# Weighted sums of two chunks over halves of 64 keys, beside scores and maxima on the other array tiles

## The reference

```
layer 0: window attention (7x7 windows, 8 heads of 8, cosine similarity, position bias), + x,
         group norm, relu; group norm, 64 -> 256 -> 64 perceptron, + h, group norm, relu  = z
layer 1: qkv = w_qkv z                    (4 heads of 16, n = m = 3136 positions)
         attn = softmax(q^T k * 16^-0.5)  (3136 x 3136 for each head and image)
         out = w_proj (v attn^T) + z
```

## Time and profile before

| | us |
|---|---|
| median of 3 runs (9116.72 to 9124.28) | 9118.54 |
| profiled execution, its own time | 9125.05 |
| its span | 9123.3 |
| TensorE matmuls busy | 8091.4 (89%) |
| VectorE busy | 7403.4 (81%) |
| ScalarE busy | 6195.0 (68%) |
| GpSimd busy | 792.9 (9%) |

### The profile page before, as it was taken

One profiled execution on the slowest core, in us unless ns is written; L12 is line 12 of the kernel. 1 busy time (PEld: TensorE's weight loads), 2 busy tenths in 40 slices (PEclk: granted clock), 3 DMA queues, 4 the chain that ended last, 5 costly groups with the idle time before them and its releaser, 6 DMA issues.

```text
span 9123.3 us, 325558 instructions
## 1 busy us (share of the span) xinstructions
PE 8091.4 (89%) x145928; PEld 2803.4 (31%) x145928; DVE 7403.4 (81%) x9252; ACT 6195.0 (68%) x13810; POOL 792.9 (9%) x677
## 2 busy tenths in 40 slices
PE   4798989989899898998989899898998989899897
PEld 2232323323233232323323233232332323233222
DVE  3788888878888788887888888788887888888884
ACT  1377667767667677676776677676776776767776
POOL 3100101001010010101001010010100101010000
PEclk8799999999999999999999999999999999999998
DMA  1201111020110201112011110201102011110110
GB/s 31 40 13 25 26 29 27 14 38 16 23 27 15 39 14 26 26 20 35 12 26 26 29 27 14 38 15 25 26 14 39 14 26 26 23 32 12 29 21 18
DMA packets 126086, 222.76 MB, mean 24 GB/s; under 512 B 60419, under 2 KB 92291, under 8 KB 124555
## 3 DMA queue, kind: packets, MB, share of 16 engines
q1 hardware_dynamic: 124690, 201.94, 12.3%
HBM read 67.50 MB, written 42.73 MB: 12 GB/s over the span
## 4 chain that ended last, share of the span: by engine, by line
PE 56%; DVE 27%; SPq 5%; DMA 4%; ACT 4%; issue 3%; POOL 0%; POOLq 0%; ACTq 0%; DVEq 0%
DVE small L949 22%; PE PS L1324 18%; PE PS L1311 15%; PE PS L1169 9%; ACT exps L842 3%; SPq L626 3%; PE PS L1210 3%; PE PS L1230 3%; DMA small<-scratch_att 1%; DVE small L988 1%; PE PS L1262 1%; PE PS L1271 1%; DMA tok_unit<-in_query_ident 1%; DMA scratch_att<-o_st 1%; PE PS L1200 1%
## 5 line engine op out<-in xcount | busy, mean ns | idle before, releaser
L842 ACT ACTIVATE exps<-PS 128x392 f32<-128x392 f32 x12800 | 5417.0, 502 | 2428.1 <-PE PS L1311 1972.0
L949 DVE TENSOR_REDUCE small<-PS 128x1 f32<-128x784 f32 x6400 | 5863.8, 965 | 895.7 <-PE PS L1169 864.5
L1311 PE MATMUL PS<-q_stack,k_stack 50*32 50x392 f16 x51200 | 3037.4, 338 | 383.7 <-DMA q_stack<-neg_rows 220.2
L1324 PE MATMUL PS<-exps,v_all 128*32 128x392 f32 x25600 | 2823.1, 516 | 11.6 <-ACT exps L842 6.6
L1169 PE MATMUL PS<-k_stack,q_stack 48*32 48x392 f16 x51200 | 2486.7, 342 | 374.3 <-DVE small L949 293.1
L1311 PEld LDWEIGHTS PS<-q_stack,k_stack 50*32 50x32 f16 x51200 | 989.1, 90 | 2528.1 <-ACT exps L842 1942.1
L1169 PEld LDWEIGHTS PS<-k_stack,q_stack 48*32 48x32 f16 x51200 | 771.2, 90 | 2039.0 <-DVE small L949 1551.9
L1324 PEld LDWEIGHTS PS<-exps,v_all 128*32 128x32 f32 x25600 | 518.8, 109 | 796.5 <-issue 491.5
L742 POOL TENSOR_TENSOR win_scores<-win_scores,small 128x784 f32<-128x784 f32 x256 | 385.1, 1506 | 1822.0 <-DVE small L1000 1822.0
L988 DVE TENSOR_REDUCE small<-PS 128x16 f32<-128x784 f32 x256 | 247.4, 966 | 187.1 <-PE PS L1210 187.0
L1210 PE MATMUL PS<-kmask,tok_unit 113*64 113x392 f32 (+1 forms) x2048 | 375.2, 502 | 19.7 <-DMA tok_unit<-in_query_ident 18.4
(11 more groups left out here) (124 smaller groups left out, 2977.3 us busy)
## 6 DMA issues: line engine op xcount, KB each, us to landing
q_stack<-tok_qk SPq DMA_DIRECT2D x256, 98.0 KB, 4.1
k_stack<-tok_qk SPq DMA_DIRECT2D x256, 98.0 KB, 4.3
kmask<-tok_unit SPq DMA_DIRECT2D x1024, 12.2 KB
att<-scratch_att SPq DMA_DIRECT2D x68, 196.0 KB
z_half<-scratch_z SPq DMA_DIRECT2D x34, 392.0 KB, 6.9
inv_sums<-scratch_rden SPq DMA_DIRECT2D x272, 49.0 KB, 2.1
scratch_att<-o_st SPq DMA_DIRECT2D x512, 26.0 KB
out<-inv_sums SPq DMA_DIRECT2D x68, 196.0 KB, 3.2
```

Of the source, the lines that this page charges most:

```text
L842: nc.scalar.activation(exps(u), PS[:, u % SCORE_BANKS, 0:GTOK], ACT.Exp, scale=score_scale).then_inc(s_exps, 1)
L949: nc.vector.tensor_reduce(max_parts[:, n_:n_ + 1], slot(), op=ALU.max, axis=AX.XY)\
L1311: last = mm(PS[32 * r:32 * r + 32, u % SCORE_BANKS, 0:GTOK], k_stack[rows, h, k0:k0 + 32], q_stack[rows, h, c * GTOK:(c + 1) * GTOK], star ...
L1324: last = mm(PS[32 * j:32 * j + 32, PV_BANK, 0:GTOK], v_all[:, stage // 2, kt, :], exps(4 * quad + j), start=(kt == 0), stop=(kt == TILES - 1))
```

## The change

- A stage of four chunks becomes two legs of two chunks. `weigh` takes two chunks of one key tile (a duo) and splits the 128 keys into two halves of 64: keys 0 to 63 on the lower rows and columns 0 to 63 of the array, keys 64 to 127 on the upper rows and columns 64 to 127. These are four tiles of 64 x 32. There are 400 weighs an image, of four fp32 matmuls each.
- `score` and `max` use the other four tiles: key groups 0 and 1 take the upper rows, groups 2 and 3 the lower. The eight matmuls of a maximum now go bank by bank, two after each other on each tile.
- The two halves of the sums are stored apart (scratch_parts) and added after they are loaded: on GpSimd (`asum`) for the numerators, on VectorE for the denominators.
- Bank 7 is copied at the end of each of 16 legs, by ScalarE. Each leg is stored with four transfers.
- `follow` counts two lanes (weighs; scores and maxima) that run beside each other, and lets the queue go on after 30 ns. Both orders are new. The start of the run has the old order.

```diff
 def weigh(duo, b):
-    for j in range(4):
-        last = mm(PS[32 * j:32 * j + 32, PV_BANK, 0:GTOK], v_all[:, stage // 2, kt, :],
-                  exps(4 * quad + j), start=(kt == 0), stop=(kt == TILES - 1))
+    for s in range(2):
+        for j in range(2):
+            p0 = CH * s + 32 * j
+            last = mm(PS[p0:p0 + 32, PV_BANK, 0:GTOK], v_all[side(s), leg // 4, kt, :],
+                      exps(2 * duo + j)[side(s), :], start=(kt == 0), stop=(kt == TILES - 1))
     last.then_inc(s_pv_done, 1)
...
+def rows_of(r, count):
+    first = CH * (r < 2)
+    return slice(first, first + count)
 def score(u, b):
-    rows = slice(CH * (j % 2), CH * (j % 2) + STACK + SHIFT)
     for r in range(4):
-        k0 = kt * 128 + 32 * r
+        k0, rows = kt * 128 + 32 * r, rows_of(r, STACK + SHIFT)
         last = mm(PS[32 * r:32 * r + 32, u % SCORE_BANKS, 0:GTOK],
                   k_stack[rows, h, k0:k0 + 32], q_stack[rows, h, c * GTOK:(c + 1) * GTOK],
...
 max:
-    for r in range(4):
-        for j in range(2):
-                      q_stack[CH * j:CH * j + STACK, stage // 2, q0:q0 + 32],
+    for j in range(2):
+        for r in range(4):
+                      q_stack[rows, stage // 2, q0:q0 + 32],
...
+def copy_leg(leg, b):      # on ScalarE, 16 an image; before copy_half on VectorE, 8 an image
+    act.wait_ge(s_pv_done, (b * LEGS + leg + 1) * TILES)
...
+    nc.scalar.activation(o_st[:, leg % 2, :], PS[:, PV_BANK, 0:GTOK], ACT.Copy).then_inc(s_out_copied, 1)
...
 IMAGE_ORDER, first and last letters
-    "MssMsMsssMWssMsMssWMssMssMWMsssMsMssWMMssWsssMs ... ssMMssWsMssMssWMMsssWssMMsssWssMsMWW"
+    "MMsssMssMWssWsMssMWssWMsMWsssWMssMssWWMsWsMsssM ... WsMsWsWMWMWH"
```

More of the change, by code:

```diff
@@ L44 @@
 PARTS = {
-    "score": (("PE", 167),), "exp": (("ACT", 380),), "weigh": (("PE", 664),),
-    "max": (("PE", 334), ("DVE", 884)), "shift": (("PE", 160), ("DVE", 220), ("SP", 2260)),
-    "copy": (("DVE", 560),), "store": (("SP", 1240),),
+    "score": (("PE", 165),), "exp": (("ACT", 378),), "weigh": (("PE", 656),),
+    "max": (("PE", 330), ("DVE", 882)), "shift": (("PE", 160), ("DVE", 220), ("SP", 3000)),
+    "copy": (("ACT", 400),), "store": (("SP", 1240),),
     "xload": (("SP", 1100),), "xorder": (("POOL", 500),),
@@ L69 @@
         "kload": 2500, "queries": 2500, "shift": 3000}
-SWITCH = 100
-SHAPES = {(128, 32): ("score", "max", "weigh", "sum", "wpv"), (128, 64): ("wscore", "wproj", "mlp2"),
+SWITCH = 110
+ISSUE = 30
+TILED = (64, 32)
+LANE = {"score": 0, "max": 0, "weigh": 1}
+SHAPES = {TILED: ("score", "max", "weigh"), (128, 32): ("sum", "wpv"), (128, 64): ("wscore", "wproj", "mlp2"),
           (64, 128): ("qk", "wval", "mlp1", "gqk", "gv"), (128, 128): ("spread", "wtrans", "gn", "final", "shift")}
@@ L150, in layer0_needs @@
     for h in range(3):
-        left = [at("weigh", (2 * h + 2) * TILES - 1)] if attended else []
+        left = [at("weigh", (4 * h + 4) * TILES - 1)] if attended else []
         step(at("stack", h), *all_of("gqk", SIDE), *all_of("piece_s", SIDE), *left)
@@ L174, in attention_needs @@
     for u in range(UNITS):
-        stage, tile = divmod(u // 4, TILES)
+        duo = u // 2
+        leg, tile = divmod(duo, TILES)
         needs[at("score", u)] = [(at("exp", u - SCORE_BANKS), None)] if u >= SCORE_BANKS else []
-        if u % (4 * TILES) == 0 and stage:
-            needs[at("score", u)].append((at("shift", stage), None))
+        if u % (4 * TILES) == 0 and leg:
+            needs[at("score", u)].append((at("shift", leg // 2), None))
         needs[at("exp", u)] = [(at("score", u), None)]
         if u >= EXP_RING:
[L181 to L188, removed]
+            needs[at("exp", u)].append((at("weigh", duo - EXP_RING // 2), None))
+        if u % 2 == 1:
+            needs[at("weigh", duo)] = [(at("exp", u), None)]
+            if tile == 0 and leg:
+                needs[at("weigh", duo)].append((at("copy", leg - 1), None))
+    for leg in range(LEGS):
+        needs[at("copy", leg)] = [(at("weigh", leg * TILES + TILES - 1), None)]
+        needs[at("store", leg)] = [(at("copy", leg), None)]
     needs[at("store", 0)] += [(at("sums", 0), None), (at("sums", 1), None)]
@@ L258, in follow @@
     assert len(tensor) == engine.count(0)
-    ready, free, shape, placed = [0] * len(tasks), [0] * 5, (128, 32), 0
+    ready, free, shape, placed = [0] * len(tasks), [0] * 5, TILED, 0
+    lanes = [0, 0]
     offered = [[n for n in range(len(tasks)) if not missing[n] and engine[n] == e] for e in range(5)]
@@ L281, in follow @@
             placed += 1
-            duration += SWITCH * (SHAPE[kind] != shape)
+            ended = duration + max([begin] + (lanes if SHAPE[kind] != shape else
+                                              [lanes[LANE[kind]]] if kind in LANE else lanes))
+            ended += SWITCH * (SHAPE[kind] != shape)
+            free[0] = begin + ISSUE if SHAPE[kind] == shape else ended - duration + ISSUE
+            for lane in [LANE[kind]] if kind in LANE else range(2):
+                lanes[lane] = ended
             shape = SHAPE[kind]
@@ L407, in attention_mlp_kernel @@
         neg_rest = small[:, 308:333]
-        sums_compact = [small[:, 336:385], small[:, 448:497]]
+        sums_compact = [small[:, 560 + 98 * k:658 + 98 * k].rearrange("p (s n) -> p s n", s=2) for k in range(2)]
         inv_compact = [small[:, 392:441], small[:, 504:553]]
```

206 lines of the change are left out of this document (112 added, 94 removed).

## The result

The changed kernel takes 9179.7 us (median of four runs, 9179.6 to 9181.2) against 9119.8 for the kernel before beside it: ratio 1.0066, interval 1.0048 to 1.0083. It is slower by 0.7%, more than the 0.2% that can be told apart; forecast were 8575 us and a range that ends at 9020.

What follows compares the result with a forecast made beforehand. No engine was always the bound; TensorE set the pace in attention-only stages, and the bound was to move to VectorE. Fifteen images at -35.5 us (-532), last image -16, end +5: -543, about 8575 us; range 8270 to 9020.

Steps and rivals of the forecast that it cites:

- TensorE's work, lanes side by side: Attention holds TensorE about 276 us if lanes run side by side; 389 us per image in all, under VectorE's 461.
- 1, the copy: Per full image, the copy out of the accumulator leaves VectorE, 16 copies come to ScalarE, hidden: -4 us.
- 2, the 15.3 us wait: VectorE's wait behind SP's stack transfers and shift goes with the new order: -13.5 us per image, bounds -15.3 and 0.
- 3, the seam: Between images, the last shift is now the order's last letter, little covers it: +5 us per image, bounds +2 and +8.
- 4, SP's issues: SP issues 16 stores of four instead of 8, and 16 loads at the seam: +2 us per image, 0 to +6.
- the end: End of the run: eight more issues ahead of the reciprocals, +5 us.
- 5, the small idle times of VectorE: Of 71.5 us per image a third goes with shape changes and blocking weighs: -25 us, bounds 0 and 60.
- rival (a): Late reports behind weighs and TensorE's program-order waits keep the small idle times; about 8950 us, chance 0.22.
- The last image: Five attention stages fall from 51.2 to about 48.5 us, -13.5; two at ScalarE's pace -1.5 each; first stage 0: -16.
- The start: Start of the run, before the first image: no change, 0 us.

Runs made afterwards that it cites:

- The first kernel: The changed kernel with one letter moved: the H of the next image's stage 0 stands 26 scores ahead of the image's end; 9169.5 us.
- the fifth kernel: The changed kernel with the 16 stores of ones moved behind the last stack of the start; 9149.9 us, ratio 1.0026 to the kernel before.
- the third kernel: The changed kernel with each weigh doing only one of its two chunks from the second key tile on; 9100.9 us, ratio 0.9974 to the kernel before.
- the sixth kernel: The kernel before with exponentials and values of the weighted sum in fp16; 9567.9 us, ratio 1.0486 to the kernel before.

## Why the prediction was wrong, point by point

The forecast was made against the profile: 9125 - 543 = 8582 us; the span and its surroundings came to 9179. Of the 597 between, these are the terms.

- **TensorE's work, lanes side by side:** right, as the timeline shows. That the bound would move to VectorE was not: its share stayed at 81%.
- **1, the copy:** it left VectorE as forecast, yet VectorE's busy time per image fell by 0.5 us only (460.8 to 460.3). The maxima, 5863.8 and now 5901.8 us in the run, take back 2.4 per image: at the same 0.97 us each, fewer overlap the one before.
- **2, the 15.3 us wait:** right; stage 5 lost 15.4 us.
- **3, the seam:** +8.5 per image instead of +5, above the bound of 8. The first kernel shows that as a cause it is worth only 0.7 per image, since VectorE waits for the stack behind it instead; so the term is not to be added to the others.
- **4, SP's issues:** +2 forecast; the 5.7 us wait of the second reciprocal has no row left in the image. At the end SP's loads of the sums take 14.3 us instead of 5.3, and the end grew by 9.3 instead of 5.
- **5, the small idle times of VectorE: the step that failed.** Forecast -25 per image from 71.5, bounds 0 and -60. Measured 86.3 (92.9 us of idle time without the 6.6 at the seam), so +15, and +19 on the waits for maxima alone. The forecast named the mechanism (a score is reported "with the weigh"), took the late end, and then argued that the two customers' cover is just enough except where two weighs stand together, so that it was priced as a smaller gain. The runs showed in its place that late reports add 32 us per image to VectorE's waits, more than twice the 13 by which its other small waits for maxima fell. But there are now 400 weighs per image and not 200, one to every two scores, and the scores late by 0.3 us and more are a quarter of all, not those behind 55 pairs. A chance of 0.22 stood on rival (a), which is this cause; its 8950 us was too low because it left the small idle times as they were.
- **The last image:** +3.1 instead of -16. The five attention stages that were to fall from 51.2 to 48.5 us take 54.3 in the mean, and the last two 5.4 together more than before. That the sum is only 3.1 is luck: stage 0, for which nothing was forecast, fell from 65.6 to 49.5.
- **The start:** +37 instead of 0: eight more stores at the start were not priced; the fifth kernel gives 30 of it back.

Start 37, images 537, last image 19 and end 4 make 597. Within an image VectorE's account closes: 0.5 less busy, the waits of 15.3 and 5.7 gone, 6.6 new at the seam and 14.8 more in small idle times make -0.1, from 553.3 to 553.2 us.

What the change is worth apart from its order: with orders from one search, 8825.4 without and 8449.2 with it, so 376 us or 4.3% for the lanes (and what comes with them, the gone copy and the queue's new positions), while the better order alone gives the kernel before 300. The forecast's 543 us for the structure would have been too much even with a good order. Still open: the larger part of why the third kernel gained 0.9%, and what the lanes are worth in the last image, since the kernel before never had a new LAST_ORDER. Whether the kernel before would gain from reports in time at a full clock wasn't shown, as the sixth kernel lost its clock.

## What to carry to other kernels

Parallel tiles shorten TensorE's work, but here a result was seen only when everything ahead of it in program order had been: price the slowest group ahead of each short one, not the short one, and put a slow group where its followers' consumers have work left. A written order is part of a structural change; fit it with reports in program order, and compare structures only with orders fitted in the same way. Count every new transfer of the start on the queue that issues it, and at the rate of a full burst.

## What the runs showed of the hardware that was not expected

- fp16 and fp32 matmuls on different row halves start 0.05 to 0.07 us apart, and both row halves write one PSUM bank at once (different partitions of it) without a later report (0.365 us for a score, as before).
- Groups that wait for the report of one ahead of them are reported behind it, mostly 59 ns apart. The kernel before shows a late report within a group: 556 maxima, whose last matmul started early on a free half, were reported 530 to 550 ns after it instead of 385.
- Less work on TensorE can cost its clock: with fp16 weighs in the kernel before, the granted clock is 0.661 instead of 0.956 and the time 4.9% longer, in all four runs; the fourth kernel, with fp16 weighs in lanes, kept 0.968. What makes the difference, no run shows.
- What a store costs SP depends on how many went before it: of stores of 17 rows of 1568 fp32 elements, issued one behind another, the first six took 0.23 to 0.97 us each and the next ten 2.6 to 5.3 (44.61 us for sixteen, 12.73 for the eight before).
